# Three attention layers and a GEGLU: the joint of layers one and two in another order, with the first layer's front and end

## What is computed

```python
# x [8, 256, 160], ctx [8, 512, 256]; all fp32
# first layer: 20 heads of 8; queries from x, keys and values from ctx
text, ip = ctx[:, :77], ctx[:, 77:]           # 77 and 435 rows
out = attend(q, k_text, v_text) + attend(q, k_ip, v_ip)  # two softmaxes
x = out @ Wo.T + bo + x
# transformer block: 20 heads of 64
n = layer_norm(x); x = x + attention(n, n)    # second layer, self attention
n = layer_norm(x); x = x + attention(n, ctx)  # third layer, cross attention
h, gate = split(layer_norm(x) @ w1 + b1)
x = x + (h * gelu(gate)) @ w2 + b2
```

## Time and profile before

| | |
|---|---|
| runs | 1478.13, 1479.65, 1481.38 us (median 1479.65) |
| profiled execution | 1479.6 us, of which the span of instructions 1477.8 |
| mean granted clock of PE | 0.991 of full speed |
| PE busy | 1448.8 us, 98% |
| VectorE busy | 1065.7 us, 72% |
| ScalarE busy | 784.7 us, 53% |
| GpSimd busy | 463.3 us, 31% |

### The profile page before, as it was taken

One profiled execution on the slowest core, in us unless ns is written; L12 is line 12 of the kernel. 1 busy time (PEld: TensorE's weight loads), 2 busy tenths in 40 slices (PEclk: granted clock), 3 DMA queues, 4 the chain that ended last, 5 costly groups with the idle time before them and its releaser, 6 DMA issues.

```text
span 1477.8 us, 40867 instructions
## 1 busy us (share of the span) xinstructions
PE 1448.8 (98%) x17914; PEld 1149.7 (78%) x17914; DVE 1065.7 (72%) x1511; ACT 784.7 (53%) x1079; POOL 463.3 (31%) x406
## 2 busy tenths in 40 slices
PE   9999999998999999999999999999999999999999
PEld 7556656567888888888787888888788888878899
DVE  7788887846777777776677676776767677686776
ACT  4777777853564456654354444544444454443444
POOL 3455457531232223433122222222222222222210
PEclk9999999998999999999999999999999999999999
DMA  4433344211000200001010100101010030000000
GB/s 136 128 84 85 83 134 121 47 30 31 2 2 2 100 2 6 2 15 46 24 30 2 30 1 2 30 1 31 2 30 2 2 77 2 2 2 2 2 14 23
DMA packets 32508, 50.43 MB, mean 34 GB/s; under 512 B 7697, under 2 KB 20945, under 8 KB 31953
## 3 DMA queue, kind: packets, MB, share of 16 engines
q1 hardware_dynamic: 32336, 47.88, 11.7%
HBM read 29.18 MB, written 1.31 MB: 21 GB/s over the span
## 4 chain that ended last, share of the span: by engine, by line
PE 85%; DVE 5%; ACT 5%; POOL 3%; issue 2%; DMA 1%; SPq 0%; ACTq 0%; POOLq 0%; DVEq 0%
PE a_pj L1047 8%; PE a_pj L1035 6%; PE l_px L1745 5%; PE a_pj L541 5%; PE a_pv L1069 4%; PE l_pst L1649 4%; PE a_px L1069 4%; PE a_px L584 3%; PE a_px L1090 3%; PE a_pscore L968 3%; PE a_pj L550 3%; PE ff_ph L2249 3%; PE a_px L570 2%; ACT l_probs L1862 2%; PE a_pst L989 2%; PE a_pv L570 2%
## 5 line engine op out<-in xcount | busy, mean ns | idle before, releaser
L1334 POOL TENSOR_TENSOR a_key_sum<-a_probs 128x512 f32<-128x512 f32 x120 | 162.9, 1362 | 443.3 <-ACT a_probs L1155 443.3
L1237 DVE TENSOR_REDUCE a_negmax<-a_pscore 128x2 f32<-128x1024 f32 x160 | 195.6, 1222 | 82.7 <-PE a_pscore L968 82.4
L1155 ACT ACTIVATE a_probs<-a_pst 128x1024 f32<-128x1024 f32 x160 | 164.2, 1026 | 140.2 <-PE a_pst L995 140.2
L2012 DVE TENSOR_REDUCE l_negmax<-l_pscore 128x2 f32<-128x154 f32 x320 | 199.9, 685 | 41.5 <-PE l_pscore L1634 41.0
L1862 ACT ACTIVATE l_probs<-l_pst 128x1024 f32<-128x1024 f32 x160 | 164.0, 1025 | 56.7 <-PE l_pst L1649 54.9
L768 POOL TENSOR_TENSOR a_key_sum<-a_probs 128x1024 f32<-128x1024 f32 x40 | 96.9, 2423 | 219.5 <-ACT a_probs L632 219.5
L708 DVE TENSOR_REDUCE a_negmax<-a_pscore 128x4 f32<-128x1024 f32 x80 | 97.6, 1220 | 40.5 <-PE a_pscore L499 40.5
L1047 PE MATMUL a_pj<-a_wv_hi,a_ct 128*128 128x256 f32 x640 | 111.9, 287 | 1.0
L632 ACT ACTIVATE a_probs<-a_pst 128x1024 f32<-128x1024 f32 x80 | 82.0, 1024 | 38.0 <-PE a_pst L525 38.0
L720 DVE RECIPROCAL a_recip<-a_pv 128x256 f32<-128x256 f32 x40 | 70.3, 1757 | 42.9 <-PE a_pv L575 42.8
L1262 DVE RECIPROCAL a_recip<-a_pv 128x256 f32<-128x256 f32 x40 | 70.2, 1756 | 42.9 <-PE a_pv L1078 42.9
(11 more groups left out here) (273 smaller groups left out, 3618.4 us busy)
## 6 DMA issues: line engine op xcount, KB each, us to landing
l_rb<-l_recip SPq DMA_DIRECT2D x40, 128.0 KB
l_ct<-in_ctx_t SPq DMA_DIRECT2D x8, 512.0 KB, 4.1
l_k_stack<-l_k_hi SPq DMA_DIRECT2D x64, 64.0 KB, 2.1
a_ct<-in_ctx_t SPq DMA_DIRECT2D x8, 512.0 KB, 4.7
a_ct<-in_ctx_t SPq DMA_DIRECT2D x16, 256.0 KB, 5.3
l_q_stack<-l_q_hi SPq DMA_DIRECT2D x80, 32.0 KB, 1.9
a_raw_wv<-in_a_wv SPq DMA_DIRECT2D x2, 1280.0 KB, 9.1
l_x<-in_x_t SPq DMA_DIRECT2D x8, 256.0 KB, 3.9
```

What stands on the lines that cost most here:

```text
L1155: nc.scalar.activation(probs[:, 2 * i:2 * i + 2, 2 * n:2 * n + 2, :], pst[:].rearrange("p h (k q) -> p h k q", k=2), ACT.Exp, scale=SCALE) ...
L1237: nc.vector.tensor_reduce(to, pscore[:], AX.X, ALU.max, negate=True).then_inc(max_done, 1)
L1334: nc.gpsimd.tensor_tensor(key_sums[n][:, two], probs[:, two, 2 * n, :], probs[:, two, 2 * n + 1, :], ALU.add).then_inc(half_summed, 1)
L2012: last = nc.vector.tensor_reduce(to[:, :, k], pscores[s % 2][:, :, keys], AX.X, ALU.max, negate=True)
```

## The change

Eight edits, all of order or of who issues; the arithmetic is the same.

1. Second layer's opening: ScalarE's copies of `wv` are spread over steps 36 to 38 (`WV_HI` counts from step 24), GpSimd's remainders come one step later.
2. `queries_keys` can run in halves (queries, keys).
3. Third layer: `sum_keys` is cut in two; the sums of keys 0 and 1 stand before the norm's work in a step, the third behind it.
4. Front: the tables of steps 0 to 4 are dealt anew; the first exponentials have a table of their own; ScalarE issues the query moves of groups 0 to 2 in place of SyncE; a `fill` has 6 or 8 products instead of 4.
5. End of the first layer: `invert_last` takes 3 groups and then 2, before 4 and 1 (`SOON`); the spreads of batch 7's first three groups stand one step earlier in SyncE's list, behind group 38's `move_dens`.
6. GpSimd splits inputs before it rounds a stack, where a step has both.
7. The weights `wq` and `wk` are loaded at steps 21 and 26 instead of both at 24.
8. The joint's order on PE, ScalarE and VectorE: a projection's half between two transposed scores, all sums of group 38 together, the second layer's first scores and values between. ScalarE's list, left out below, follows PE's.

```diff
...
-    WV_HI = [(12, 0), (12, 1), (12, 3), (13, 0), (13, 1), (13, 3)]
+    WV_HI = [(12, 3), (13, 0), (13, 1), (13, 3), (14, 1), (14, 3)]
...
-        def queries_keys(d):
+        def queries_keys(d, halves=range(2)):
             b, u = divmod(d, STEPS)
-            if d == 0:
+            if d == 0 and 0 in halves:
                 pe.wait_ge(*ahead["max_done"])
...
                 pe.wait_ge(wv_done, 4)
-            if u == 0:
+            if u == 0 and 0 in halves:
                 pe.wait_ge(ln.n_ready, b + 1)
-            wait(pe, v_copied, d)
-            for which, w in enumerate((wq, wk)):
+            if 0 in halves:
+                wait(pe, v_copied, d)
+            for which in halves:
+                w = (wq, wk)[which]
                 for k, (ws, hl, s) in enumerate(N_ROWS):
...
                                   nts[b % 2][OWN[t], hl, s, :], start=k == 0, stop=k == len(N_ROWS) - 1)
-            last.then_inc(qk_ready, 1)
+            if 1 in halves:
+                last.then_inc(qk_ready, 1)
...
-        return dict(part=part, rest=rest)
+        return dict(part=part, rest=rest, score=score, queries_keys=queries_keys)
...
                 nc.gpsimd.memset(ones[:], 1.0).then_inc(ones_set, 1)
-            if k == 12:
+            if k == 13:
                 pool.wait_ge(wv_hi, 2)
                 low(wv, 0).then_inc(wv_done, 1)
-            if k == 13:
+                ln.pool_lo(pool, 0, nts[0])
+            if k == 14:
                 pool.wait_ge(wv_hi, 4)
                 low(wv, 1).then_inc(wv_done, 1)
-                ln.pool_lo(pool, 0, nts[0])
-            if k == 14:
+            if k == 15:
+                pool.wait_ge(*ahead["biased"])
                 pool.wait_ge(wv_hi, 6)
...
     def gpsimd(pool):
-        def sum_keys(e):
-
-            wait(pool, pv_done, e)
-            for n in range(2):
+        def sum_keys(e, halves=range(2)):
+
+            if 0 in halves:
+                wait(pool, pv_done, e)
+            for n in halves:
                 for i in range(2):
...
         def step(d):
+            if here(d - 2):
+                sum_keys(d - 2, [0])
             if norm_at(d, LN_STATS):
...
             if here(d - 2):
-                sum_keys(d - 2)
+                sum_keys(d - 2, [1])
...
-    EARLY = {(0, 0): ("v3", 0), (0, 1): ("ip", 1), (0, 2): ("v0", 1), (1, 0): ("text", 1), (1, 2): ("v1", 1),
-             (2, 3): ("q", 1), (3, 2): ("v2", 1), (3, 3): ("rest", 1), (4, 2): ("v3", 1)}
-    FILLED = {(0, 3): (8, ("ip", 1)), (1, 1): (4, ("v0", 1)), (1, 3): (8, ("v1", 1)), (2, 0): (4, ("v1", 1)),
-              (2, 1): (6, ("v1", 1)), (2, 2): (4, ("v1", 1))}
+    EARLY = {(0, 0): ("v3", 0), (0, 2): ("ip", 1), (0, 3): ("v0", 1), (1, 2): ("text", 1), (1, 3): ("v1", 1),
+             (2, 2): ("q", 1), (2, 3): ("v2", 1), (3, 2): ("v3", 1), (3, 3): ("rest", 1)}
+    FILLED = {(0, 0): (8, None), (0, 3): (4, ("ip", 1)), (1, 0): (6, ("v0", 1)), (1, 1): (8, ("v0", 1)),
+              (1, 2): (4, ("v0", 1)), (2, 0): (6, ("v1", 1)), (2, 1): (8, ("v1", 1))}
+    FIRST_EXPS = {(1, 2): (0, 0), (1, 3): (0, 1), (2, 0): (0, 2), (2, 1): (0, 3)}
+    FIRST_SCORES = {(0, 0): (0, 1), (0, 1): (), (0, 2): (2,), (0, 3): (3,)}
     PLAN = {(0, 2): ("v3", 0), (0, 3): ("ip", 1), (1, 2): ("text", 1), (1, 3): ("q", 1), (2, 2): ("v0", 1),
...
+    def exp_at(t, s):
+        if t <= T_LAG:
+            return FIRST_EXPS.get((t, s))
+        return (t - T_LAG, s) if here(t - T_LAG) else None
+
+
     def in_pj(use):
...
+    SOON = 3
...
+    ACT_MOVED = 3
+
+
+    def move_queries(eng, u):
+        main = u < GROUPS - 1
+        rows = slice(u * ROWS, (u + 1) * ROWS) if main else slice(0, ROWS)
+        for r, half in enumerate(Q_ROLES):
+            eng.dma_start(q_stack[r:P:4, u, :], q_n[half][rows, 0 if main else 1].bitcast(FP32)).then_inc(
+                stacked[u], 16)
+
     def sync(sp):
...
             wait_rounded(sp, GROUPS * (m - 1) + u)
-            main = u < GROUPS - 1
-            rows = slice(u * ROWS, (u + 1) * ROWS) if main else slice(0, ROWS)
-            for r, half in enumerate(Q_ROLES):
-                sp.dma_start(q_stack[r:P:4, u, :], q_n[half][rows, 0 if main else 1].bitcast(FP32)).then_inc(
-                    stacked[u], 16)
+            move_queries(sp, u)
...
             sp.dma_start(den[u * DENS:(u + 1) * DENS, m % 2, :],
-                         sums[0:P:P // DENS, m % 2, u, :]).then_inc(end_den_in if g == ALL - 1 else den_in[m % 2], 16)
+                         sums[0:P:P // DENS, m % 2, u, :]).then_inc(end_den_in if g >= ALL - GROUPS + SOON else den_in[m % 2], 16)
...
             wait(sp, multiplied, m)
-            for u in range(GROUPS if m < B - 1 else GROUPS - 1):
+            for u in range(GROUPS if m < B - 1 else SOON):
                 spread_group(u).then_inc(spread_in, 16)
...
             sp.wait_ge(recip_done, B + 1)
-            spread_group(GROUPS - 1).then_inc(end_spread_in, 16)
+            for u in range(SOON, GROUPS):
+                spread_group(u).then_inc(end_spread_in, 16)
...
             for group in range(2):
-                stack_queries(0, group)
                 stack_keys(0, group)
...
                 stack_keys(0, group)
-                stack_queries(0, group)
+                if group >= ACT_MOVED:
+                    stack_queries(0, group)
             load_first(sp)
...
                 spread_recips(b - 2)
-            if t == STEPS0 - 1:
-                spread_recips(B - 1)
             if here(t - V_LAG):
                 move_dens(t - V_LAG)
+            if t == STEPS0 - 2:
+                spread_recips(B - 1)
             if u == 2 and b + 1 < B:
...
             k = k4[:, (t - 1) % GROUPS]
-            for _ in range(4):
+            for _ in range(8 if s == 3 else 6):
                 mm((pj if s == 3 else px)[:, 0:SQ], k[:, 0:P], k[:, 0:SQ], start=True, stop=True)
...
-            bank, read, uses = (pj, pj_read, pj_uses) if in_pj(use) else (px, px_read, px_uses)
-            pe.wait_ge(read, uses[use] + 1)
+            bank, read, uses = (pj, pj_read, pj_uses) if use is None or in_pj(use) else (px, px_read, px_uses)
+            if use:
+                pe.wait_ge(read, uses[use] + 1)
             for _ in range(n):
...
             pe.wait_ge(px_read, len(px_uses))
-            for k, groups in enumerate((range(GROUPS - 1), [GROUPS - 1])):
+            for k, groups in enumerate((range(SOON), range(SOON, GROUPS))):
                 pe.wait_ge(last_done, k + 1)
...
-            if here(t) and not V_LAG <= t < ALL - GROUPS:
+            if t >= ALL - GROUPS and here(t):
                 score(t, s)
-            if here(t - T_LAG):
-                turned_scores(t - T_LAG, s)
+            if exp_at(t, s):
+                turned_scores(*exp_at(t, s))
+            if t < V_LAG:
+                for k in FIRST_SCORES.get((t, s), (s,)):
+                    score(t, k)
             if V_LAG <= t < ALL - GROUPS and s % 2 == 0:
...
-        return dict(begin=begin, part=part, output_last=output_last)
+        return dict(begin=begin, part=part, output_last=output_last, sums=weighted_sums,
+                    turned=lambda t, s: turned_scores(*exp_at(t, s)))
...
                     take_first(what)
+                if what == "text":
+                    act.wait_ge(zeroed, 2)
+                    act.wait_ge(q_low, 1)
+                    move_queries(nc.scalar, 0)
...
             copy(q4[:, 0, :], q_stack[:, 0, :]).then_inc(first_rounded, 1)
+            for u in range(1, ACT_MOVED):
+                move_queries(nc.scalar, u)
...
         def part(t, s):
-            if here(t - T_LAG):
-                exp(t - T_LAG, s)
+            if exp_at(t, s):
+                exp(*exp_at(t, s))
             if s == 1 and here(t - V_LAG):
...
-            n = (GROUPS - 1) * DENS
             if k == 0:
-                dve.wait_ge(den_in[(B - 1) % 2], DENS_IN * (B // 2) - 16)
+                dve.wait_ge(den_in[(B - 1) % 2], DENS_IN * (B // 2) - 16 * (GROUPS - SOON))
                 dve.wait_ge(spread_in, DENS_IN * (B - 1))
             else:
-                dve.wait_ge(end_den_in, 16)
-            rows = slice(0, n) if k == 0 else slice(n, n + DENS)
+                dve.wait_ge(end_den_in, 16 * (GROUPS - SOON))
+                dve.wait_ge(spread_in, DENS_IN * B - 16 * (GROUPS - SOON))
+            rows = slice(0, (SOON if k == 0 else GROUPS) * DENS)
             nc.vector.reciprocal(recip[rows, :], den[rows, (B - 1) % 2, :]).then_inc(recip_done, 1)
...
             if k == 0:
-                dve.wait_ge(spread_in, DENS_IN * B - 16)
+                dve.wait_ge(spread_in, DENS_IN * B - 16 * (GROUPS - SOON))
                 dve.wait_ge(multiplied, B - 1)
...
             else:
-                dve.wait_ge(end_spread_in, 16)
-            parts = ((slice(0, 2), rb[0][:]), (slice(2, 4), rb[1][:, 0:2, :])) if k == 0 else ((slice(4, 5), rb[1][:, 2:3, :]),)
+                dve.wait_ge(end_spread_in, 16 * (GROUPS - SOON))
```

(83 more changed lines are left out.)

26 lines of the change are left out of this document (17 added, 9 removed).

## The result

The changed kernel takes 1461.38 us in the median of four runs (1458.41 to 1462.23) beside 1478.89 for the kernel before (1477.29 to 1481.38): ratio 0.9884, 95% interval 0.9855 to 0.9913. The forecast was 1460.8. The profiled execution took 1460.72, its span 1458.9, 18.9 less than before.

The account below looks back on a forecast made before the run. PE was taken as the bound, busy 1448.8 of 1477.8 us, so only its waits, half-clock time or path could be cut. 1479.6 - 6.6 - 11.0 - 1.3 + 0.4 - 0.3 = 1460.8, range 1452 to 1470.

Parts of the forecast that it names:

- the key sums: Third layer, steps with a norm's statistics: two key sums moved before the norm's work end PE's wait, -6.6 us.
- the rest: Steps 36 and 37 at the half clock -0.5, step 38's copies +0.2: -0.3 us in all.
- the seam: First layer's end and second's start: new order shortens PE's waits, 45.7 us wide to 34.7, -11.0 us.
- the weights: Step 28: with no weight load before the spreads, GpSimd's output product starts 1.3 us earlier, -1.3 us.
- the front: Steps 0 to 5: more fills delay step 3, most returns at step 5's full clock, net +0.4 us.
- the six steps: Sign: the third layer's steps with a norm's statistics take 15.9 to 16.1 us.
- step 28: Sign: still some 3 us too long, with ScalarE's copy waiting about 2 us for `l_ot`.
- step 3: Sign: starts about 2 us later, 2.2 in the reckoning, from ten more fills and a projection of values.
- rival B: Third layer: key sums stay late, VectorE slowed beside GpSimd, PE still waits 0.6; gain 3.0, total 1464.4, chance 0.13.
- a dip of the clock: First layer's end and second's start: 1.2 us added for one more clock drop after PE's 1.3 us wait.
- Rival E: Step 28: loads issued behind the spreads slow them as before, the 4.3 us stay; total 1462.1, chance 0.06.
- the half clock near step 4: Placed at step 5 by the prediction: half clock should go, 8.6 - 7.1 = 1.5 us back.

Follow-up runs that it names:

- the old order: The changed kernel with the three engines' old order of the joint, three groups still inverted early: 1467.33 us in one run.
- the run with `wv` beside the spreads: The changed kernel with one key sum before the norm's work instead of two, and four loads issued by ScalarE at steps 31 and 32: 1462.57 us.
- the kernel before, run a second time: The kernel before with only the third layer's key sums cut in two, its first two layers unchanged: 1472.7 us against 1477.7, ratio 0.9968.
- one sum ahead: The changed kernel with one of the three key sums before the norm's work instead of two: 1455.3 us first, 1456.01 in five rounds, ratio 0.9851.

## Why the prediction was right, term by term

The total was hit because misses of both signs cancelled: the key sums and the rest gave 3.7 us less than forecast, the seam, the weights and the front 3.9 more. That is luck. The mechanism of the largest term, the seam, held. Three of the signs that the prediction named did not come: the six steps took 16.3 us and not 15.9 to 16.1, step 28 was 0.8 us too long and not 3, and step 3 started 1.07 us later and not 2.

**Key sums:** forecast 6.6, measured 4.1 in six steps (4.8 in the layer). The step that failed is "VectorE is then held by its own maxima and not by GpSimd": the moved second sum fell on VectorE's statistics and cost 0.44 us a step. That is rival B's mechanism at a lower price (0.44, not 0.6), in a place that B did not name; the row that I had set against the edit was the right warning, and the moved work should have been laid beside every VectorE instruction of its new place, not only beside the maxima.

**Seam:** forecast 34.7 us wide, measured 34.0. The chain followed held to a microsecond: the last denominators issued at 321.75 (forecast: after the three spreads, +16.2 from 306.3, 322.5), landed at 326.4 (+20.4, 326.7), PE's one long wait 1.47 us (1.3). The 1.2 us for a dip of the clock were not needed: it stayed at 1.00. What the experiments add is the price of the deal of three and two, which the prediction did not give by itself: 6.0 us in the old order and 3.4 in the new.

**Weights:** forecast 1.3, measured 3.5. The product came 2.5 us earlier and not 1.3, and the step that failed is that each microsecond of lateness costs one: the table of leads shows 3.3 us that come or go as a whole at a lead between 1.1 and 1.4. That this execution stood on the short side, by at most 0.5 us, was luck too; with the same loads two of eleven did not. The measured 3.5 lies inside the bounds of 0 and 4.3. Rival E did not come true for `wq` and `wk`, but the run with `wv` beside the spreads shows its mechanism at 4.4 us. A likely reason, not tested: in the changed kernel `wq` and `wk` go out some 3 us after the last spread of the batch before them (176.79 after 173.74, 213.48 after 210.58), while `wv` went out 0.9 after it (246.89 after 246.03).

**Front:** forecast +0.4, measured -0.5, by two errors. Step 3 starts 1.07 us later instead of 2.2: ten fills and a projection more cost half of what their rows say one by one, and why was not tried. And the 1.5 us for the half clock near step 4 were credited to the change, while the kernel before, run a second time, did not have it: against that execution the front costs 1.0 us. ScalarE's nine issues, for which no row had a price, took 6.4 us together (forecast 5).

**The rest:** forecast -0.3, with -0.5 for steps 36 and 37 and +0.2 for step 38. Step 36 measured -1.3, which the second execution of the kernel before had without the change; step 38 measured +2.8. This was not among the rivals. PE had gained 5.3 us by step 38, but the product of batch 5 hangs on SyncE's queue and started at 286.59, before at 286.11. Timelines of the changed kernel:

```profile
286.59 3.05 POOL L2205 TENSOR_TENSOR l_ot<-l_rb,l_sums 128x512 f32<-128x512 f32 x2 [8.97 <-DMA l_rb<-l_recip]
...
289.67 0.38 ACT L1850 ACTIVATE l_sums<-l_px 128x256 f32<-128x256 f32 x1 [1.33 <-POOL l_ot L2205]
...
290.11 0.97 PE L1783 MATMUL l_px<-l_k 128*128 128x256 f32 x6 [0.79 <-ACT l_sums L1850]
...
292.08 3.00 PE L1807 MATMUL l_pj<-l_wo,l_ot 128*128 128x160 f32 x10
```

I had read that SyncE is late at step 28 and stopped there. The question that was missing is where PE meets the same queue next. The run with `wv` on ScalarE's queue at step 33 settles it: with the product 1.2 to 1.4 us earlier than with one sum ahead, step 38 takes 7.56. Its lead there is 3.0; with leads of 2.4, 2.0 and 1.6 (one sum ahead twice, the changed kernel) step 38 took 8.02, 8.37 and 10.39. ScalarE's copies, for which I had put 0.2, cost nothing in that run.

Two versions have lower medians than the changed kernel's 1461.4: one sum ahead, 1456.01, and the same with `wv` loaded by ScalarE at step 33, 1456.08. Their ratios' intervals overlap with the changed kernel's (0.9855 to 0.9913), so their times alone do not set them apart; the 2.6 us in the third layer are shown by the steps.
